# Softmax sums of the second layer on ScalarE and its divisions on GpSimd, keys spread by ScalarE, values in four quarters of the array

## The reference, cut to what matters

```python
x = x + tanh(g_xattn[0]) * L0_xattn(layernorm(x), ctx)   # 16 heads of 64, 4 heads of keys and values
x = x + tanh(g_ffn[0])   * L0_ffn(layernorm(x))          # 16 heads of 8, plus a mixture of 8 experts
x = x + tanh(g_xattn[1]) * L1_xattn(layernorm(x), ctx)   # 16 heads of 8, masked
x = x + tanh(g_ffn[1])   * L1_ffn(layernorm(x))          # mixture of experts
x = x + tanh(g_xattn[2]) * L2_xattn(x, ctx)              # 4 heads of 32, rotary, masked
x = x + tanh(g_ffn[2])   * L2_ffn(layernorm(x))          # experts by sorted tokens
x = x + tanh(g_xattn[3]) * L3_xattn(layernorm(x), ctx)   # 16 heads of 64
x = x + tanh(g_ffn[3])   * L3_ffn(layernorm(x))

# every attention: q = x Wq, k = src Wk, v = src Wv, split into heads
attn = softmax(q k^T * scale)            # over the 64 keys of a sequence
out = (attn v) joined over heads @ Wo    # the second layer has no Wo
# second layer: attn_out + sum over the two best experts of gate * (x We + be)
```

## Time and profile before

| what | value |
|---|---|
| median of 3 executions | 4557.56 us (4556.44 to 4560.14) |
| profiled execution, its own time | 4552.95 us |
| its span, first to last instruction | 4551.1 us |
| mean granted clock of PE | 0.866 of full |
| busy: PE, PEld | 3947.3 us (87%), 3104.3 us (68%) |
| busy: DVE, ACT, POOL | 3006.2 us (66%), 1735.9 us (38%), 764.9 us (17%) |

### The profile page before, as it was taken

The page is one execution under the profiler, slowest core; times in us unless marked ns, Lnnn a source line. Parts: engine busy times, 40 slices in busy tenths (PEclk is TensorE's granted clock), DMA queues, the critical chain, the costliest instruction groups (busy, mean ns, idle before and its releaser), DMA issues.

```text
span 4551.1 us, 105680 instructions
## 1 busy us (share of the span) xinstructions
PE 3947.3 (87%) x36890; PEld 3104.3 (68%) x36890; DVE 3006.2 (66%) x9082; ACT 1735.9 (38%) x4156; POOL 764.9 (17%) x575
## 2 busy tenths in 40 slices
PE   6999978888886888889999999777737899999965
PEld 4888855555554555589999999655537777777754
DVE  4666657777775777766666666799861355555569
ACT  3555534444442344333333333222203344444421
POOL 1222221111110000011111111100171122222211
PEclk9999987777776677689999999888758999999975
DMA  3000010000001000000000000100015200000000
GB/s 124 8 7 8 7 23 6 6 6 6 6 7 65 16 16 15 15 6 0 0 0 0 0 0 3 44 12 12 6 39 191 98 12 12 9 12 12 10 13 26
DMA packets 102053, 97.04 MB, mean 21 GB/s; under 512 B 31664, under 2 KB 91056, under 8 KB 101296
## 3 DMA queue, kind: packets, MB, share of 16 engines
q1 hardware_dynamic: 97408, 76.94, 5.6%
q0 software_dynamic: 4096, 8.40, 0.6%
q10 hardware_dynamic: 432, 10.19, 0.6%
HBM read 46.97 MB, written 19.66 MB: 15 GB/s over the span
## 4 chain that ended last, share of the span: by engine, by line
PE 60%; DVE 18%; SPq 8%; issue 7%; POOL 2%; DMA 2%; ACT 1%; DVEq 1%; POOLq 0%; ACTq 0%
PE ps L768 54%; SPq L591 7%; PE ps L936 5%; DVE acc L1658 2%; DMA arena_a<-kT 1%; DVE o_sb L1637 1%; POOL scr L718 1%; PE ps L806 1%; DVE arena_b L1606 1%; POOL route L740 1%; DVE xn L1442 1%; DVE x_sb L1557 1%; DVE st L1401 1%; DVE mx L1527 1%; DVE vsmall L1614 1%
## 5 line engine op out<-in xcount | busy, mean ns | idle before, releaser
L768 PE MATMUL ps<-xcT,small 128*128 128x256 f32 x2176 | 610.1, 419 | 34.7 <-DMA xcT<-in_ctxT 25.4
L732 POOL TENSOR_TENSOR rstd<-veps,neghalf 128x2 f32<-128x2 f32 (+1 forms) x224 | 167.9, 749 | 2403.8 <-DVE veps L1434 2071.2
L768 PEld LDWEIGHTS ps<-xcT,small 128*128 128x128 f32 x2176 | 411.3, 204 | 233.3 <-issue 114.5
L768 PE MATMUL ps<-arena_b,qT 64*64 64x64 f32 (+3 forms) x11136 | 541.8, 242 | 21.6 <-DVE arena_b L1606 20.3
L1278 ACT ACTIVATE kT<-ps 128x256 f32<-128x256 f32 (+1 forms) x768 | 294.4, 383 | 623.6 <-PE ps L768 547.4
L768 PE MATMUL ps<-small,xcT 128*64 128x64 f32 (+5 forms) x3072 | 482.7, 384 | 51.4 <-DVE acc L1658 30.3
L768 PE MATMUL ps<-xhi,parts_a 128*128 128x256 f32 (+1 forms) x2112 | 500.4, 289 | 22.7 <-DVE qT L1687 22.7
L768 PEld LDWEIGHTS ps<-arena_b,qT 64*64 64x64 f32 (+3 forms) x11136 | 463.5, 149 | 58.4 <-issue 35.0
L1248 ACT ACTIVATE pT<-ps 128x512 f32<-128x512 f32 (+1 forms) x576 | 303.3, 571 | 467.0 <-PE ps L936 465.3
L1687 DVE TENSOR_TENSOR qT<-kT,ps 128x256 f32<-128x256 f32 (+1 forms) x768 | 316.8, 419 | 188.5 <-ACT kT L1278 181.0
L768 PE MATMUL ps<-xlo,parts_a 128*128 128x256 f32 (+1 forms) x1536 | 430.6, 280 | 0.0
(11 more groups left out here) (212 smaller groups left out, 6388.5 us busy)
## 6 DMA issues: line engine op xcount, KB each, us to landing
wbuf<-parts_b SPq DMA_DIRECT2D x39, 512.0 KB, 3.0
arena_a<-kT SPq DMA_DIRECT2D x1024, 8.0 KB
xcT<-in_ctxT SPq DMA_DIRECT2D x96, 128.0 KB, 2.1
xn<-scr SPq DMA_DIRECT2D x39, 128.0 KB, 2.2
scr_y<-acc SPq DMA_DIRECT2D x39, 128.0 KB, 2.9
scr<-vsmall SPq DMA_DIRECT2D x9, 512.0 KB, 13.3
ctx_sb<-in_ctx SPq DMA_DIRECT2D x32, 128.0 KB, 2.1
arena_a<-in_w ACTq DMA_DIRECT2D x1, 4096.0 KB, 12.4
```

Of the source, the lines that this page charges most:

```text
L732: pool.tensor_tensor(rstd[:, 0:n], veps[:, 0:n], neghalf[:, 0:n], ALU.pow).then_inc(s_rstd.sem, 1)
L768: return nc.tensor.matmul(o, lhsT, rhs, start=start, stop=stop, skip_group_check=True)
```

## The change

It has four parts.

- Second layer: each exp also gives the sum of its 64 results (accum_out). DVE takes the reciprocals in stage N, POOL multiplies probs in stage N, T waits for POOL, the ones are left out of the values, and stage A on DVE is an addition of acc and one residual in place of a reciprocal, two multiplications and two residuals. In the built program a second ACT instruction, which reads the accumulator, follows each of these exps (16 a tile).
- Second and third layers: k_spread has 8 slots for 16. ACT writes all of them from PSUM, with a scale that is one for a head's own partitions and zero elsewhere (own_head), and a bias to match. kT, the 16 DMAs, their semaphore and the two memsets of zeros go; five small DVE instructions make own_head and head_bias.
- First and seventh layers: values use all four 64x64 quarters of the array. The second sequence of a tile lands on the other half of the partitions; ACT copies each bank in two 64x512 instructions, and W is 16 matmuls with 64 columns of weights, of which the second sequence's use a wo whose halves are swapped.
- SP loads that swapped wo into arena_b with two DMAs at the start, and again with two for the seventh layer ahead of the first expert tile.

```diff
+        wo_swapped = arena_b[:, 6144:7168]
...
         def k_spread(par):
-            return arena_a[:, par * 4096:(par + 1) * 4096].rearrange("p (h t) -> p h t", h=16)
+            return arena_a[:, par * 4096:par * 4096 + 8 * GT].rearrange("p (h t) -> p h t", h=8)
...
+            def swap_wo(src, a, b):
+                for half in range(2):
+                    sp.dma_start(wo_swapped[half * S:(half + 1) * S, :],
+                                 src[(1 - half) * S:(2 - half) * S, a:b]).then_inc(s_swap, 16)
...
             sp.dma_start(x_sb[:, 0:n, :], x_v[:, 0:n, :]).then_inc(s_x0, 16)
             sp.dma_start(small[:, 0:FIRST_W], small_in[:, 0:FIRST_W]).then_inc(s_small, 16)
...
+            swap_wo(small_in, *SMALL_AT["l0x_wo"])
...
-                    sp.wait_ge(drained[layer.front_ring.bank(g, 1)], layer.front_ring.count(g, 1))
-                    for h in range(16):
-                        sp.dma_start(k_spread(g.par)[8 * h:8 * h + 8, h, :],
-                                     kT[8 * h:8 * h + 8, g.par, :]).then_inc(s_kspread.sem(g), 16)
...
+                a = LATE.index("l3x_wo") * 1024
+                swap_wo(late_in, a, a + 1024)
...
-                if layer is L0F:
-                    for b in L0X.body_banks:
-                        pool.wait_ge(drained[b], bank_base[1][b])
-                    pool.memset(arena_a[:, 0:4096], 0.0).then_inc(s_zero, 1)
...
-                if item[0] == "N" and layer in (L0X, L3X):
+                if item[0] == "N" and layer in (L0X, L0F, L3X):
...
-                blocks = [(0, hb) for hb in range(2)] if layer is L0X else [(i, hb) for i in range(4) for hb in range(2)]
-                for turn in ((0, 1), (1, 0)):
-                    halves = (0, 1) if turn == (0, 1) else (1, 0)
-                    for i, hb in blocks:
-                        for half in halves:
-                            j = turn[half]
-                            rows = slice(half * S, (half + 1) * S)
-                            if layer is L0X:
-                                last = mm(bank(banks[j])[rows, hb * 256:(hb + 1) * 256],
-                                          v_heads(layer, g.par)[rows, 2 * t + hb, j, :],
-                                          pT[rows, t, 4 * j:4 * j + 4, hb * S:(hb + 1) * S])
-                            else:
-                                last = mm(bank(banks[j])[rows, i * P + hb * S:i * P + (hb + 1) * S],
-                                          v_heads(layer, g.par)[rows, 2 * t + hb, 4 * j + i, :],
-                                          pT[rows, t, 4 * j + i, hb * S:(hb + 1) * S])
-                            if turn == (1, 0) and (i, hb) == blocks[-1]:
-                                last.then_inc(filled[banks[j]], 1)
+                n = 2 if layer is L0X else 8
+                for c, half, hb in itertools.product(range(n), range(2), range(2)):
+                    rows = slice(half * S, (half + 1) * S)
+                    to = slice((half ^ hb) * S, ((half ^ hb) + 1) * S)
+                    w0, heads = 512 // n, 8 // n
+                    last = mm(bank(banks[half])[to, c * w0:(c + 1) * w0],
+                              v_heads(layer, g.par)[rows, 2 * t + hb, c, :],
+                              pT[rows, t, c * heads:(c + 1) * heads, hb * S:(hb + 1) * S])
+                    if (c, hb) == (n - 1, 1):
+                        last.then_inc(filled[banks[half]], 1)
...
-                        if layer in (L0F, L1X):
-                            pe.wait_ge(s_kspread.sem(g), s_kspread.all(g))
...
-                                          k_spread(g.par)[rows, 8 * half:8 * half + 8,
-                                                          t * P + hb * S:t * P + (hb + 1) * S])
+                                          k_spread(g.par)[rows, :, t * P + hb * S:t * P + (hb + 1) * S])
...
                     t = item[1]
-                    if layer in (L0X, L3X):
+                    if layer in (L0X, L0F, L3X):
                         pe.wait_ge(s_probs.sem, s_probs.after(g, t))
-                    elif layer is L0F:
-                        wait_drained(layer.score_ring, g, t)
                     else:
                         pe.wait_ge(s_exp.sem, s_exp.after(g, t))
...
-                                last = mm(o[:, c * 36:(c + 1) * 36], pT[:, t, c, :],
-                                          v_small(g.par)[:, 2 * t:2 * t + 2, c, :])
+                                e = 16 if layer is L0F else 18
+                                last = mm(o[:, c * 2 * e:(c + 1) * 2 * e], pT[:, t, c, :],
+                                          v_small(g.par)[:, 2 * t:2 * t + 2, c, 0:e])
...
+                    if chunks == 8:
+                        for c in range(8):
+                            for hb in range(2):
+                                toks = slice(hb * S, (hb + 1) * S)
+                                wo = w(layer.name + "_wo") if hb == 0 else wo_swapped
+                                last = mm(bank(b)[toks, 0:D], oT[:, t, c, toks], wo[:, c * D:(c + 1) * D],
+                                          start=c == 0, stop=c == 7)
+                        last.then_inc(filled[b], 1)
+                        return
...
-                    act.wait_ge(s_kspread.sem(g.back(2)), s_kspread.all(g.back(2)))
                     nc.scalar.activation(qT[:, g.par, 0, :], bank(b, GT), ACT.Identity,
                                          bias=w(layer.name + "_bq"))
-                    nc.scalar.activation(kT[:, g.par, :], bank(b)[:, GT:2 * GT], ACT.Identity,
-                                         bias=w(layer.name + "_bk")).then_inc(drained[b], 1)
+                    for h in range(8):
+                        last = nc.scalar.activation(k_spread(g.par)[:, h, :], bank(b)[:, GT:2 * GT], ACT.Identity,
+                                                    bias=head_bias[:, layer.n - 1, h:h + 1],
+                                                    scale=own_head[:, h:h + 1])
+                    last.then_inc(drained[b], 1)
...
                     for h in range(layer.heads):
                         last = nc.scalar.activation(probs[:, g.par, t, h * S:(h + 1) * S],
                                                     score_bank(b)[:, h * S:(h + 1) * S], ACT.Exp,
-                                                    bias=negmax[:, t, h:h + 1], scale=layer.scale)
+                                                    bias=negmax[:, t, h:h + 1], scale=layer.scale,
+                                                    accum_out=sm[:, t, h:h + 1])
...
                     for j in range(2):
                         b = wait_filled(ring, g, u + j)
-                        if layer is L0X:
-                            o = oT[:, t, 4 * j:4 * j + 4, :].rearrange("p i (b q) -> p b i q", b=2)
-                            i = bank(b).rearrange("p (b i q) -> p b i q", b=2, i=4)
-                        else:
-                            o = oT[:, t, 4 * j:4 * j + 4, :].rearrange("p c t -> p (c t)")
-                            i = bank(b)
-                        nc.scalar.activation(o, i, ACT.Copy).then_inc(drained[b], 1)
+                        for hb in range(2):
+                            rows = slice((j ^ hb) * S, ((j ^ hb) + 1) * S)
+                            last = nc.scalar.activation(oT[rows, t, :, hb * S:(hb + 1) * S],
+                                                        bank(b)[rows, :].rearrange("p (c q) -> p c q", q=S), ACT.Copy)
+                        last.then_inc(drained[b], 1)
...
                         v18 = vsmall[rows, :, :].rearrange("p a (n e) -> p a n e", e=18)
                         dve.memset(v18[:, :, :, 16 + half:17 + half], 1.0).then_inc(s_ones, 1)
+                    dve.tensor_reduce(den[:, 0, 0:16], ident.rearrange("p (h d) -> p h d", d=8), AX_X,
+                                      ALU.add).then_inc(s_heads0, 1)
+                    dve.wait_ge(s_heads0, 1)
+                    dve.tensor_tensor(own_head[:, :], den[:, 0, 0:8], den[:, 0, 8:16], ALU.add).then_inc(s_heads0, 1)
+                    dve.wait_ge(s_heads0, 2)
+                    for i, bk in enumerate(("l0f_bk", "l1x_bk")):
+                        dve.tensor_scalar(head_bias[:, i, :], own_head[:, :], w(bk), None, ALU.mult).then_inc(s_heads, 1)
...
-                if layer in (L0F, L1X, L2X):
+                if layer in (L1X, L2X):
+                    return
+                if layer is L0F:
+                    wait_drained(layer.score_ring, g, t)
+                    dve.reciprocal(rv[:, t, 0:nh], sm[:, t, 0:nh]).then_inc(s_rv.sem, 1)
                     return
...
                     e = 16 if layer is not L2X else 64
                     c = 8 if layer is not L2X else 2
+                    if layer is L0F:
+                        src = bank(b, c * 2 * e).rearrange("p (c b e) -> p c b e", b=2, e=e)
+                        wait_drained(fr, g, layer.use(("Z", t)))
+                        for half in range(2):
```

(12 more changed lines are left out.)

25 lines of the change are left out of this document (14 added, 11 removed).

## The result

The changed kernel takes **4630.97 us** (median of 4, 4629.99 to 4631.64) beside 4558.85 us for the kernel before on the same chip (4 runs, 4556.44 to 4560.16): ratio 1.0159, 95% interval 1.0141 to 1.0176, 72 us slower. Forecast were 4600 and slower, in a range of 4510 to 4700. Sign and range held. Two terms of the sum did not: the third layer was put at 0 and costs 90 us, and the second was put at +96 and costs 35. The two errors have opposite signs, and that they largely cancel is luck.

What follows compares the result with a forecast made beforehand. TensorE alone was taken to bound the first and seventh layers, chains through several engines the second and third. Terms -17 - 38 + 0 + 96 + 2 = +43 on 4553 gave 4596, forecast 4600; range 4510 to 4700.

Steps and rivals of the forecast that it cites:

- Values in the first layer: First layer, four-quarter values: 0.9 us less a tile, A0's gain lost as a wait; -0.5 us a group, -17 us.
- Values in the seventh layer: Seventh layer, four-quarter values: A1 starts 0.6 us sooner and is 0.95 shorter, projections +0.4; -1.2 us a group, -38 us.
- Rival 4: First and seventh layers: the four evacuations do not overlap and bound both; +38 us, 4638 in all, chance 0.07.
- Keys in the third layer: Third layer, keys spread by ScalarE: taken as 0, between +22 us from waits and -26 us from a faster clock.
- Net +0.7 us a group: Third layer: T0's evacuation 1.6 us later behind the key copies, less 0.90 us TensorE idle removed; +22 us.
- rival 3: Third layer: the keys pay because the clock comes back sooner; -26 us, 4574 in all, chance 0.13.
- Sums and keys in the second layer: Second layer: key copies and exps with read-outs on ScalarE delay the meta copy; +3.0 us a group, +96 us.
- The sign named in advance: Second layer: Z0 waiting for the meta copy, exps over 10 us a group, groups 26 us apart.
- Rival 1: Second layer: accumulator reads hide in the pipe, 0.27 us a head; +35 us there, 4540 in all, chance 0.20.
- rival 2: Second layer: reads do not overlap, 0.42 us a head, or the clock halves in waits; +136, 4694, chance 0.20.
- What it saves ... nothing: Second layer: VectorE work saved, a residual a tile and half a reciprocal, lies ahead of V's evacuation; gains 0.
- Once only: One-time costs: swapped wo loads, 2.3 us at the start and about 2 before expert tiles, memsets -2.5; together +2 us.

Runs made afterwards that it cites:

- v_sums: Kernel before plus four-part values and, in the second layer, sums on ScalarE and divisions on GpSimd; keys still by DMA: 4498.31 us, ratio 0.9863.
- v_order: Changed kernel with the third layer's next-group query and key projection (QK) moved behind T1: 4491.66 us, ratio 0.9851 to the kernel before.
- v_four: Changed kernel with only four of the eight key copies in the third layer, so half its heads are wrong: 4518.34 us (1 run).
- v_mixed: Changed kernel with QK behind T1 in the third layer and the second layer's keys by DMA again: 4437.03 us, ratio 0.9732 to the kernel before.
- v_values: Kernel before with only the four-part values of the first and seventh layers: 4519.35 us, ratio 0.9912.
- v_shift: Kernel before with the four-part values and one unused 24-column tile declared ahead of the others in memory: 4507.71 us (1 run).
- v_dma_order: v_sums with QK of the third layer moved behind T1, keys still by DMA: 4603.49 us (1 run).

## Why the prediction was right or wrong

**Values in the first layer: right, the size near.** Forecast -17 with +2 at the start, measured -9. In the steady part a group goes from 17.66 to 17.22 us, -0.44 against -0.5; the slower first context tile costs 2.0 (the interval behind it goes from 31.2 to 33.2 us) against 2.3. The rest is in the layer's first and last groups; over the kernels with the same first layer its length varies from 603 to 611 us, so a few us there mean nothing. The parts: the values save 0.85 us a tile (0.9 forecast); 0.83 us a group come back as waits, most of them at another stage than forecast, and with the lost overlap around them A0's gain is more than gone (+0.98 against +0.9); the records of the projection cost 1.96 us a tile and not 2.19, but with their edges the projections are 0.28 us a group dearer (+0.4 forecast).

**Values in the seventh layer: right.** -35.7 against -38, values 1.16 us a tile, as worked out from the score records. A steady group is 1.35 us shorter, against -1.2: the stage ahead of A1 grows by 0.56 us as worked out (0.6), and the projections cost nothing where +0.4 was forecast; the layer's first and last groups give some of it back. Rival 4 and the statement beside it, that the evacuation may become the bottleneck (the Trainium skill, TensorEngine Tiling (Array Packing), PSUM Bottleneck), hold in part: four evacuations of 64x512 take 2.27 us where 4 x 0.6 = 2.4 was the upper bound, they overlap, and they return a part of TensorE's gain in either layer, not all of it.

**Keys in the third layer: wrong, and by mechanism.** The failed step is "Net +0.7 us a group", with "I take 0, between the two". It had the right wait, T1 behind pT behind the copies. It took it for 1.6 us less the 0.9 of idle that goes, and took the clock for a possible gain. The runs show 2.66 us of wait, since S1 and T0 now come sooner and at full clock and so TensorE reaches T1 earlier, while pT still stands behind the copies; the clock came back one step sooner, as rival 3 had it, was spent on S1 and the wait, and was gone for A0 and A1. These went from 4.0 us a group (118.8/30 in v_sums, whose third layer is that of before) to 6.9 (206.2/30). In 30 groups (v_sums, then the changed kernel) the wait for pT grows from 7.7 to 79.8 us and A0 and A1 by 87.4; on the other side the scores' wait for the DMA, 33.9 us, is gone, and a record of the scores costs 193 ns in place of 217 (91.1/472, 105.0/484) and one of QK 397 in place of 513 (46.1/116, 61.6/120). Together a steady group grows from 16.9 to 20.45 us. v_order and v_four show both halves: with the wait gone A0 and A1 are at 3.66 us again, and with the wait cut to 0.8 us they are halfway. The beginning of the layer gives 13 us back (its second and third groups took 26.4 and 17.5 us and take 17.3 and 13.1), which leaves the 90. Rival 3, the keys pay, holds only with QK moved (v_order, -58 us, and v_mixed, -48.5).

**Sums and keys in the second layer: the mechanism right, the size too large.** +34.8 against +96. The sign named in advance is there: Z0 waits 2.5 us for the meta copy. But ScalarE's exps take 9.3 us a group where over 10 were forecast, and groups are 23.9 us apart and not 26. Term by term, from the table of places (after less before, a group): first exp +2.54, forecast 3.3; exps +2.87, forecast 3.9; last exp to meta copy -2.26, to Z0 -1.42, from there -0.70, together -4.38, forecast about -4.2. Sum +1.03 in place of +3.0. So two terms were too large. The read-out costs 0.093 us (0.290 less 0.197), and I had taken 0.12, between bounds of 0.06 and 0.21. Rival 1's cheaper reads and rival 2's dearer ones both miss: the exps are 0.290 us apart, and by the forecast's own formula (E1.0 at 904.2 + 32x) that still gives +57 us and not +35. The walk was made along a quick group: in it the first exp is at 5.06 us, in the mean of 29 groups at 6.54. And it took the groups as all alike, while the changed kernel has 15 quick groups of 29 and the kernel before 9: quick ones go from 21.5 to 23.2 us and the others from 23.5 to 24.7, by more than the mean does. So the first exp moves by 3.29 us with the keys alone but by 2.54 with the sums there too. The estimate from the Trainium skill's figures (ScalarE: Activation LUTs, What ACT_TABLE_LOAD costs) was 0.094 us for the read-out, and on that the trace agrees with 0.093; the +64 us taken from it (x = 0.30 in the formula gives +67) is still too high for the same reason.

**"What it saves ... nothing" in the second layer: wrong in size.** v_sums is 23 us shorter there than v_values, where ScalarE is not last. Over half of it is that more groups are quick, and E1.0's wait for V's evacuation is halved but not gone. That the work taken from VectorE is the cause was not tested by itself.

**Once only: near.** +2.0 at the start, forecast 2.3; the sixth layer is 5.4 longer, forecast 2, of which v_values, with the same loads, shows 1.2; the rest stays open. No run shows the 2.5 us put down for the two memsets by themselves.

**Not in the forecast: the fourth layer's -9.6 us,** which v_shift gives with nothing but another place of the tiles in memory.

## What to carry to other kernels

When work moves to an engine that is far from full, its price is not its length but what stands behind it in that engine's line, and which bank or buffer it keeps: in the third layer the same eight copies cost 90 us ahead of pT and won 58 behind it, and in the second they cost 108 more when put where a PSUM bank was wanted. A wait of TensorE can also cost the clock of the run of matmuls behind it: 2.66 us ahead of T1 came with all of A0 and A1 at 1.2 GHz, 0.83 us with part of them, and 4.9 us ahead of the scores, in v_dma_order, with none. Such a run is to be priced at both clocks. And slack is to be taken as a mean over the groups of a stage, and spent once: two parts that each fit into it may not fit together.

## What the runs showed of the hardware

- An accumulator read-out behind a 128x64 exp adds 0.093 us on ScalarE; in the trace it is an instruction of its own, drawn 0.21 to 0.46 us long.
- Copies of 128x256 out of PSUM with scale and bias from memory cost 0.469 us each, drawn 0.58.
- Two sets of 128x64-weight records, each writing another half of the partitions, run at once: 1536 of them take 94 us, where 768 with 128x128 weights take 93.5.
- Records of 36 columns cost 116 ns at 2.4 GHz and 215 to 218 at 1.2 (111.3/960 in v_order; 206.2/960 and 6.99/32 in the changed kernel).
- 96 bytes in the place of the tiles change the fourth layer's matmuls of 256 columns by 1% and the kernel by about 10 us (950.8 and 939.0 us for the layer in v_values and v_shift), with no instruction changed.
